# Tridiagonalisation of a 1024 x 1024 matrix: another order of the work in the steps with one to three tiles, and waits written in another order

## What is computed

```python
deg = jnp.sum(A, axis=0) + jnp.sum(A, axis=1) - jnp.diagonal(A)
d_inv_sqrt = jnp.where(deg > 0, jax.lax.rsqrt(deg), 0.0)
L = jnp.diag(deg) - A
L_norm = d_inv_sqrt[:, None] * L * d_inv_sqrt[None, :]
_, U = jnp.linalg.eigh(L_norm)
agg = jnp.einsum('mn,bnd->bmd', U.T, features)
h = jax.nn.relu(agg @ W1 + b1)
out = h @ W2 + b2
return jnp.einsum('nm,bmd->bnd', U, out)
```

## Time and profile before

| | us |
|---|---|
| median of 3 executions | 9616.06 (9606.15 to 9617.1) |
| the profiled execution | 9610.06 |
| its span | 9608.3 |
| tridiagonalisation, from the first panel on | 838 to 5918 |
| of it steps with T = 8 to 4 | 838 to 4350 |
| of it steps with T = 3, 2, 1 | 545, 523 and 500 |

### The profile page before, as it was taken

How to read it: one execution, slowest core, us unless ns; L and a number is a source line. 1 busy time by engine, 2 the same in 40 slices (tenths; PEclk the granted TensorE clock), 3 DMA queues, 4 the chain that set the end, 5 groups by cost and what they waited for, 6 DMA issues and landing times. The chain is left out here.

```text
span 9608.3 us, 324471 instructions
## 1 busy us (share of the span) xinstructions
PE 5544.2 (58%) x136408; PEld 3923.0 (41%) x136408; DVE 7081.8 (74%) x33318; ACT 1750.2 (18%) x4677; POOL 1160.5 (12%) x5161
## 2 busy tenths in 40 slices
PE   5695888777888777777777764121111110027856
PEld 2464555555666666556666553010000000023446
DVE  3666666777777777777777778988989899974155
ACT  1441111111111111111111111121111110010036
POOL 0001111111222222222222221000000000000000
PEclk8898999999999998886665555555555555569989
DMA  1000000000000000000000000000000000000000
GB/s 36 1 1 20 4 4 4 4 4 4 4 4 4 4 4 4 4 4 4 4 4 3 3 3 2 0 0 0 0 0 0 0 0 0 0 0 0 1 18 18
DMA packets 24637, 42.49 MB, mean 4 GB/s; under 512 B 2464, under 2 KB 20128, under 8 KB 23200
## 3 DMA queue, kind: packets, MB, share of 16 engines
q1 hardware_dynamic: 23200, 21.70, 0.7%
HBM read 17.50 MB, written 4.19 MB: 2 GB/s over the span
## 5 line engine op out<-in xcount | busy, mean ns | idle before, releaser
L289 PE MATMUL tri_y<-L 128*32 128x256 f32 (+7 forms) x36792 | 1926.3, 341 | 9.0 <-issue 8.4
L289 PEld LDWEIGHTS tri_y<-L 128*32 128x32 f32 x36792 | 1192.6, 121 | 214.0 <-issue 44.8
L1370 PE MATMUL ev_agree<-ev_prod,ev_fold 128*128 128x448 bf16 x520 | 241.4, 568 | 1683.6 <-DVE ev_prod L1493 1667.0
L1370 PEld LDWEIGHTS ev_agree<-ev_prod,ev_fold 128*128 128x128 bf16 x520 | 34.7, 111 | 1888.0 <-DVE ev_prod L1493 1867.6
L314 PE MATMUL tri_ring<-ident 128*128 128x128 bf16 x7414 | 747.8, 268 | 1.4 <-issue 1.2
L1486 DVE SCALAR_TENSOR_TENSOR ev_seq<-ev_seq,ev_ne2G,ev_u 128x112 f32<-128x112 f32 x2048 | 686.0, 335 | 73.3
L1482 DVE SCALAR_TENSOR_TENSOR ev_u<-ev_x,ev_dG,ev_seq 128x112 f32<-128x112 f32 x2048 | 684.0, 334 | 64.0
L272 PE MATMUL tri_k<-tri_kp,tri_half 128*32 128x1 f32 x8176 | 264.0, 188 | 771.4 <-DVE tri_x L476 768.0
L364 ACT ACTIVATE tri_mu<-tri_ring,tri_tiny 128x1 f32<-128x1 f32 x1022 | 267.1, 261 | 2136.1 <-PE tri_ring L272 2136.1
L314 PEld LDWEIGHTS tri_ring<-ident 128*128 128x128 bf16 x7414 | 580.5, 121 | 169.1 <-issue 153.6
L366 ACT ACTIVATE tri_sM<-tri_half_M,tri_s 128x8 f32<-128x8 f32 (+7 forms) x1022 | 304.2, 298 | 1832.9 <-DVE tri_s L468 1832.9
(11 more groups left out here) (611 smaller groups left out, 12839.8 us busy)
## 6 DMA issues: line engine op xcount, KB each, us to landing
adj<-in_adj_dram SPq DMA_DIRECT2D x12, 1024.0 KB, 8.1
x<-in_x_dram SPq DMA_DIRECT2D x8, 512.0 KB, 7.3
out_dram<-x SPq DMA_DIRECT2D x8, 512.0 KB, 6.6
gcn_w<-in_L_gnn_W_dram SPq DMA_DIRECT2D x2, 128.0 KB, 2.2
spec_w<-in_L_gnn_W_dram SPq DMA_DIRECT2D x2, 64.0 KB, 1.8
dot_wt<-in_L_gnn_W_dram SPq DMA_DIRECT2D x1, 64.0 KB, 1.9
dot_rows<-in_L_gnn_b_lin_dram SPq DMA_DIRECT2D x1, 64.0 KB, 2.7
dot_rows<-in_L_gnn_b_dram SPq DMA_DIRECT2D x1, 64.0 KB, 3.6
```

Source lines behind the costliest of these rows:

```text
L289: last = nc.tensor.matmul(y[32 * g:32 * g + 32, 0:T * 32], A[:, b + t, XC:XC + 1].broadcast_to([P, 32]), cols, start=(t == 0), stop=(t == ...
L1370: last = nc.tensor.matmul(agree, fold16[:, :], prod[:, z, h * (GRP // 2):(h + 1) * (GRP // 2), :].rearrange("p s w -> p (s w)"), start=Fal ...
```

## The change

With T <= 3 (`few(T)`, 384 steps less the last one) a step is written anew; with T >= 4 the order of a few lines and waits differs.

With T <= 3: kappa is no longer a row sum on VectorE followed by one `four`; TensorE multiplies gx (as weight) with t, one `four` per tile, and does the same with `zh` = t * s4/2, made on ScalarE, into c_sum. VectorE's L476 goes, and so does its `BnS` (L462), which GpSimd now adds itself. The flag is made earlier, from a second copy of sigma (`sigma_v`), and VectorE no longer reads the bank that ScalarE reads. q is made from t under the mask and half of s4; x is made from `vmc` = vm * s4/2 and an unscaled kappa. ScalarE has five instructions per step for three. VectorE squares the new x before it writes w, not after. The multiplications into the unread bank go for T <= 3 and stay for T = 4 to 6. s4 has two columns (s4 and half of it).

With T >= 4: the flag is made after S2, not ahead of prodb; ahead of x the wait for kappa is written first; ahead of w the wait for c_sum is written first; ahead of vm the wait for inv is written first.

The diff, cut to its core:

```diff
+FILL = {6: 8, 5: 10, 4: 10}
...
+        few = lambda T: T <= 3
+        norm_first = lambda T: T <= 3
+        idle = lambda T: FILL.get(T, 0)
... GpSimd
+                        if few(T):
+                            pool.wait_ge(fl_ready, r + 1)
+                            nc.gpsimd.tensor_scalar(fB[:, b:NT], half_M[:, s, 0:T], fl[:, s:s + 1], None, ALU.mult).then_inc(pool_step, 1)
+                            pool.wait_ge(pool_step, 3 * r + 1)
+                            nc.gpsimd.tensor_tensor(nB[:, b:NT], fB[:, b:NT], half_M[:, s, 0:T], ALU.subtract).then_inc(pool_step, 1)
+                            if s:
+                                pool.wait_ge(sum_ready, r + 1 if s0 else r)
+                                nc.gpsimd.tensor_tensor(col, Cw[:, b:NT, s], rowsum[:, b:NT], ALU.add).then_inc(Bn_ready, 1)
+                                pool.wait_ge(Bn_ready, r + 1 if s0 else r)
+                            pool.wait_ge(pool_step, 3 * r + 2)
+                            nc.gpsimd.tensor_tensor(Bc[:, b:NT], nB[:, b:NT], col, ALU.mult).then_inc(pool_step, 1)
... TensorE
-                        early = 0 if T < 4 else 1
+                        first = T if T <= 2 else 1
...
                         four(sigma, ones[:, 0:32], part[:, :]).then_inc(norm_ready, 1)
+                        if few(T):
+                            four(sigma_v, ones[:, 0:32], part[:, :]).then_inc(norm_again, 1)
+                            for t in range(first):
+                                product(t)
...
-                        if T <= 6:
-                            for _ in range(8 if T == 6 else 10):
+                        for _ in range(idle(T)):
+                            nc.tensor.matmul(ring[3][:, 0:P], ident16, ident16, start=True, stop=True)
+                        if few(T):
+                            pe.wait_ge(t_ready, r + 1)
+                            pe.wait_ge(gx_ready, r + 1)
+                            for t in range(T):
+                                last = four(kappa(s), gx[:, b + t:b + t + 1].broadcast_to([P, 32]), tm[:, t0 + t:t0 + t + 1], start=(t == 0), stop=(t == T - 1))
+                            last.then_inc(kappa_ready, 1)
+                            pe.wait_ge(zh_ready, r + 1)
+                            for t in range(T):
+                                four(c_sum, gx[:, b + t:b + t + 1].broadcast_to([P, 32]), zh[:, b + t:b + t + 1], start=(t == 0), stop=False)
... ScalarE, after mu
+                            act.wait_ge(fl_ready, r + 1)
+                            nc.scalar.activation(Cf[:, b:NT], Cw[:, b:NT, s], ACT.Copy, scale=fl[:, s:s + 1]).then_inc(Cf_ready, 1)
+                        act.wait_ge(inv_ready, r + 1)
                         act.wait_ge(xm_ready, r + 1)
-                        act.wait_ge(inv_ready, r + 1)
                         nc.scalar.activation(vm[:, b:NT], xm[:, b:NT], ACT.Copy, scale=inv[:, 1:2]).then_inc(vm_ready, 1)
+                        if few(T):
+                            act.wait_ge(s4_ready, r + 1)
+                            act.wait_ge(vm_ready, r + 1)
+                            nc.scalar.activation(vmc[:, b:NT], vm[:, b:NT], ACT.Copy, scale=s4[:, s, 1:2]).then_inc(vmc_ready, 1)
+                            act.wait_ge(t_ready, r + 1)
+                            nc.scalar.activation(zh[:, b:NT], tm, ACT.Copy, scale=s4[:, s, 1:2]).then_inc(zh_ready, 1)
... VectorE, few(T): norm(r) is L430; order sg, fl, rt, prodb, S2, prodc, pair, rowsum, corr, inv, transpose, gx, t, then
+                            dve.wait_ge(fl_ready, r + 1)
+                            V_.scalar_tensor_tensor(out=s4[:, s, :], in0=one_half[:, :], scalar=inv[:, 0:1], in1=f1.broadcast_to([P, 2]), op0=ALU.mult, op1=ALU.mult).then_inc(s4_ready, 1)
+                            dve.wait_ge(t_ready, r + 1)
+                            kk = mark(V_.tensor_tensor(qa[:, act_t], tm, Mw[:, s, 0:T], ALU.mult))
+                            dve.wait_ge(Cf_ready, r + 1)
+                            dve.wait_ge(sum_ready, pre)
+                            k_f = mark(V_.scalar_tensor_tensor(out=q1[:, act_t], in0=rowsum[:, act_t], scalar=f1, in1=Cf[:, act_t], op0=ALU.mult, op1=ALU.add))
+                            dve.wait_ge(pool_step, 3 * r + 3)
+                            dve.wait_ge(s4_ready, r + 1)
+                            after(kk)
+                            kk = mark(V_.scalar_tensor_tensor(out=q[:, act_t], in0=qa[:, act_t], scalar=c4h, in1=Bc[:, act_t], op0=ALU.mult, op1=ALU.add))
+                            after(k_f)
+                            V_.scalar_tensor_tensor(out=z, in0=tm, scalar=c4, in1=colf, op0=ALU.mult, op1=ALU.add).then_inc(z_ready, 1)
+                            dve.wait_ge(kappa_ready, r + 1)
+                            dve.wait_ge(vmc_ready, r + 1)
+                            after(kk)
+                            V_.scalar_tensor_tensor(out=X, in0=vmc[:, act_t], scalar=kappa(s), in1=q[:, act_t], op0=ALU.mult, op1=ALU.subtract).then_inc(x_ready, 1)
+                            if s + 1 < s1:
+                                norm(r + 1)
+                            dve.wait_ge(c_ready, r + 1)
+                            dve.wait_ge(v_ready, r + 1)
+                            (w, as L490)
... VectorE, T >= 4
                             kk = mark(V_.reciprocal(rt[:, :], mu[:, :]))
-                        ins = V_.tensor_scalar(f1, pivot(s)[:, 1:2], pivot(s)[:, 1:2], sigma, ALU.mult, ALU.is_lt)
                             (prodb, S2 as before)
+                            ins = V_.tensor_scalar(f1, pivot(s)[:, 1:2], pivot(s)[:, 1:2], sigma, ALU.mult, ALU.is_lt)
...
-                        dve.wait_ge(vm_ready, r + 1)
                         dve.wait_ge(kappa_ready, r + 1)
+                        dve.wait_ge(vm_ready, r + 1)
                         after(kk)
                         (x, L487)
-                        dve.wait_ge(v_ready, r + 1)
                         dve.wait_ge(c_ready, r + 1)
+                        dve.wait_ge(v_ready, r + 1)
                         (w, L490)
```

More of the change, by code:

```diff
@@ L418, in _, with norm @@
                     dve.wait_ge(window_ready, pn + 1)
+                    def norm(r):
+                        if r:
+                            dve.wait_ge(x_ready, r)
+                        X = xcol(b)
+                        V_.tensor_tensor_reduce(out=x2[:, act_t], in0=X, in1=X, scale=1.0, scalar=0.0, op0=ALU.mult, op1=ALU.add,
+                                                accum_out=part[:, 0:1]).then_inc(norm_part, 1)
+                    if norm_first(T):
+                        norm(0)
                     for s in range(s0, s1):
@@ L448, in _ @@
-                        after(kk)
-                        kk = mark(V_.scalar_tensor_tensor(out=S2[:, :], in0=rt[:, :], scalar=sigma, in1=mu[:, :], op0=ALU.mult, op1=ALU.add))
-                        if s:
-                            after(k_b)
-                            k_b = mark(V_.tensor_reduce(rowsum[:, act_t], c3(prodb), mybir.AxisListType.XY, ALU.add))
-                        after(kk)
-                        kk = mark(V_.scalar_tensor_tensor(out=pair[:, s, :], in0=S2[:, :].broadcast_to([P, 2]), scalar=sg[:, :], in1=pivot(s), op0=ALU.mult, op1=ALU.add))
@@ L455, in _ @@
-                        if s:
-                            dve.wait_ge(coefs_ready, r + 1 if s0 else r)
-                            k_c = mark(V_.tensor_tensor(c3(prodc), v_w(b)[:, :, :, 0:s], spread(coefs(s)), ALU.mult))
-                        after(kk)
-                        V_.reciprocal(inv[:, :], pair[:, s, :]).then_inc(inv_ready, 1)
-                        if s:
-                            after(k_b)
-                            V_.tensor_tensor(BnS[:, s, 0:T], Cw[:, act_t, s], rowsum[:, act_t], ALU.add).then_inc(Bn_ready, 1)
-                            after(k_c)
-                            k_c = mark(V_.tensor_reduce(corr[:, act_t], c3(prodc), mybir.AxisListType.XY, ALU.add))
@@ L465, in _ @@
-                        dve.wait_ge(inv_ready, r + 1)
-                        if not s:
-                            dve.wait_ge(Bn_ready, r + 1)
-                        V_.tensor_scalar(c4, inv[:, 0:1], f1, None, ALU.mult).then_inc(s4_ready, 1)
-                        k_t = mark(V_.scalar_tensor_tensor(out=gx[:, act_t], in0=X, scalar=inv[:, 0:1], in1=H_, op0=ALU.mult, op1=ALU.add))
-                        k_t = turn()
-                        after(k_t)
-                        if s:
-                            k_t = mark(V_.tensor_tensor(tm, trc, corr[:, act_t], ALU.add))
-                            after(k_t)
@@ L482, in _ @@
-                        after(kk)
-                        kk = mark(V_.tensor_tensor(q[:, act_t], qa[:, act_t], Bc[:, act_t], ALU.add))
-                        dve.wait_ge(vm_ready, r + 1)
-                        dve.wait_ge(kappa_ready, r + 1)
-                        after(kk)
```

(3 more changed lines are left out.)

190 lines of the change are left out of this document (143 added, 47 removed).

## The result

The changed kernel takes 9571.0 us (median of 6 executions, 9556.48 to 9587.02), the kernel before 9618.78 (6 executions beside them, 9606.15 to 9628.03). The ratio is 0.9952 [0.9939, 0.9966]: 46 to 48 us are saved, where 250 were forecast, and 9571 lies above the range (9315 to 9455). The profiled execution took 9556.48, its span is 9554.8, against 9608.3 before.

A forecast was written before the change was run, and what follows sets the result against it. It took a step as VectorE's stream plus two visits to other engines. Savings of 41.5 (T >= 4), 58 (T=3), 69 (T=2) and 81 (T=1), 250 us, off 9610 gave 9360, as median 9366; range 9315 to 9455.

The forecast's parts named there:

- T=1: Steps with T=1: 3.12 us each against 3.78 over a panel, 81 us saved in the stage.
- 0.13 behind each wait: Price in steps with T <= 3: q and x each start 0.13 us after what they need.
- kappa hidden: Steps with T=1: TensorE's kappa reaches x at 1.62 us after prodb's start, in the shadow of q.
- C (semaphore instructions, ScalarE's pitch): Steps with T <= 3: added semaphore instructions and slower ScalarE pitch take 0.38 us off the saving; 9508 us, chance 0.13.
- D (GpSimd): Steps with T <= 3: GpSimd gets no turn while VectorE streams, steps 0.50 us longer; 9760 us, chance 0.04.
- Part 1: Waits ahead of w, 639 steps with T >= 4: w and the chain behind it 0.065 us earlier, 41.5 us saved.
- Rival B: Order of waits is worth nothing at T >= 4, only the new T <= 3 steps gain; 9408 us, chance 0.20.
- The Trainium skill's rule in the prediction: Between Vector instructions the semaphore costs nothing extra; by it the reordered waits at T >= 4 save 0.
- T=2: Steps with T=2: 3.36 us each against 3.93, 0.56 saved over 124 steps, 69 us.
- T=3: Steps with T=3: mean saving 0.47 us over 124 steps, 58 us, worked at the low clock.
- Rival E: Steps are not shortened, since something unseen such as instruction supply sets the pace; 9616 us, chance 0.03.
- The unread multiplications: Ten per step, removed at T <= 3: they stand where TensorE would wait, so removal gains 0.

## Why the prediction was wrong, and where it was right

**T=1 was right** in each term: -78 for -81, the step 3.09 for 3.12. The pitch of VectorE's stream, 0.13 behind each wait, kappa hidden, GpSimd in time. So the rivals C (semaphore instructions, ScalarE's pitch) and D (GpSimd) fall: at these prices nothing of theirs is in the step.

**Part 1 was wrong at "sigma, the root and the whole chain follow it", 41.5 us for 2.** The price (0.065) and w's and the square's places were right, but the chain passes through TensorE, where product(0) stands ahead of sigma at T >= 4, 0.22 long and more. I followed w on VectorE and did not look at what TensorE does between the square and the root. "Also where TensorE's products bound a step, since they queue behind sigma" failed too: the first product does not queue behind sigma, and where the products are long VectorE's transpose waits for them, before (282.1 us in 283 steps) as after. The wait over T = 8 to 4, after (127 of the steps are at T=8, 90 at T=7):

```profile
DVE tri_tr L569 <- PE tri_y L313: 282.2, 288, 3.6
```

With sigma ahead of the product at T = 4 to 6 the run gave 11 to 24 us. For T = 8 and 7 no run tried it. Rival B gave this part its right number, for another reason: not a hair of delay, but a queue. The Trainium skill's rule in the prediction (VectorE: DVE Perf Modes, "The DRAIN you can't avoid") made part 1 nothing, and nothing came at T >= 4, but by that queue. The rule's case is one signal per instruction; of several waits ahead of one instruction it says nothing, and there the run with the waits alone saved 33 us, mostly at T <= 3.

**T=2 was wrong in the size of one term, -34 for -69.** I took 0.107 for each `four` of a product. That is the pitch of a `four` over one column; with 64 columns the product took about 0.20 each (5152.84 to 5153.24 for two), with 96 columns 0.30. Two products make rows late by 2 x 0.09, and prodb came at x + 1.54, not 1.30. The run with rows first gives 23 us of the missing 35 back. Its mean step is then 3.42 where 3.36 was worked out, 8 of the last 12 us; the rest lies between the panels.

**T=3 was wrong in kind: +60 for -58.** "They cost VectorE nothing and stand where TensorE would wait, so taking them away gains 0" looks at the time of instructions. Their number counts too: a step went from 212 to 273 TensorE instructions in about 4 us, and 60.5 us of "issue" appeared. The prediction gave that no term. Rival E named instruction supply, but as a pace for all steps alike, with 0.03. It isn't one: it is lost in some steps and not in others, by their place against the packets. With the place right, and one `four` fewer, the stage is 516 to 521, a saving of 24 to 29. The rest to the 58 lies between x and prodb: 3.61 was the quickest step after, where s=3 was to take 3.27. From prodb to x it took 2.30 (3.77 - 1.47, the kernel shifted by 130), as the 2.29 that I worked out for s=20; but prodb came at x + 1.47, not 1.20 to 1.37. In that kernel it is the flag ahead of 1/mu. In the changed kernel prodb came at x + 1.52, by the product ahead of rows: with rows first it was 1.38.

**The unread multiplications** were set at 0, and the total bears it out: putting them back at T <= 3 gave 14 us more, not less (intervals overlap). At T=2 and 1 the steps did not change (3.57 and 3.09 with and without). At T=3 "they stand where TensorE would wait" was wrong for the new step at the low clock, 4.00 for 3.65, and the high clock gave about as much back. What that clock is worth in a step without the stops no run shows. On the Trainium skill's advice to avoid PE-idle gaps (TensorE: Matmul & The Clock Gate, "Why this matters for your kernels") the trace agrees about the clock, 0.63 with them and 0.50 without at T=3; the time did not follow it.

What stays open: exactly which instruction of a packet triggers the next request, and how many TensorE still has then, so the quick and the slow places could not be forecast; and whether the up to 19 us by which T=7 differs among kernels with the same code there are the same effect.

## What to carry to other kernels

Follow a saving through every engine's queue up to the wait that it is meant to shorten; 0.065 us saved on one engine vanished behind a 0.22 us product on the next. Count an engine's instructions per loop step as well as their time: with 257 per step and steps of 4 us, where the loop starts moved this kernel by 2%; 352 in steps of 6.2 us cost nothing of the kind. When unread work is added or taken away to steer the clock, look at what stands behind it at either clock. When steps with the same work take two different times and the trace names no releaser, compare the instruction transfers with the steps before looking for a cause in the chain.

## What the runs showed of the hardware

- Instructions of TensorE came in packets of 16.4 kB, about one for each 256 of them. After a stop without a releaser it went on about 2.4 us after the packet's start; a stop cost 1.2 us on average and 1.7 at most. 121 such stops in 124 steps cost 148 us.
- The stop depended on the place: the same step took 3.77 us after a shift by 130 instructions and 5.2 with none, and was slow again after a shift by 256.
- At T=3 the granted clock was 0.63 with ten unread multiplications per step and 0.50 without; at the low clock they took 1.25 us, and the step 4.00 for 3.65.
- At the low clock (0.50, 1.2 GHz) a `four` of small f32 multiplications went from 0.107 us with one column to 0.20 with 64 and 0.30 with 96.
- Of several waits ahead of one instruction the one that comes last should be written first: with the old order in three places, the mean step with T <= 3 was 0.07 to 0.09 us longer.
